# Grouped attention in a new order: scores of the next head first, queries three heads ahead, output tiles spread over three heads

## The reference

```
bsz, q_len, _ = hidden_states.shape          # 2, 512, 512 columns
q = (hidden_states @ wq.T)...                # 32 heads of 128
k = (hidden_states @ wk.T)...; v = ...       # 8 heads of 128, each shared by 4 query heads
q = q * cos + _rotate_half(q) * sin
k = k * cos + _rotate_half(k) * sin
scores = jnp.einsum('bhqd,bhkd->bhqk', q, k) / math.sqrt(HD)
scores = scores * scale                      # 0.5 or 1.5 for some key columns
scores = scores + causal
probs = jax.nn.softmax(scores, axis=-1)
attn = jnp.einsum('bhqk,bhkd->bhqd', probs, v)
return attn @ wo.T
```

## Time and profile before

| what | value |
|---|---|
| median of 3 runs | 3551.32 us (3546.72 to 3552.46) |
| profiled execution | 3529.9 us, span 3528.1 us |
| TensorE | 2449.5 us busy, 69% |
| VectorE | 2231.0 us busy, 63% |
| ScalarE | 1390.7 us busy, 39% |
| GpSimd | 1191.0 us busy, 34% |
| mean granted clock of TensorE | 0.818 |
| weight units loaded | 442 of 256 KB |

### The profile page before, as it was taken

How to read it: one execution, slowest core, us unless ns; L and a number is a source line. 1 busy time by engine, 2 the same in 40 slices (tenths; PEclk the granted TensorE clock), 3 DMA queues, 4 the chain that set the end, 5 groups by cost and what they waited for, 6 DMA issues and landing times.

```text
span 3528.1 us, 32687 instructions
## 1 busy us (share of the span) xinstructions
PE 2449.5 (69%) x10360; PEld 1826.1 (52%) x10360; DVE 2231.0 (63%) x3359; ACT 1390.7 (39%) x2692; POOL 1191.0 (34%) x1040
## 2 busy tenths in 40 slices
PE   4885888466668467567888898888989765037026
PEld 3343377354456345446766676666767544036015
DVE  2734645798996699896435555535555444963973
ACT  1542612343431333442116555535555414713621
POOL 2020153421224421424554454545545303044030
PEclk8896998587889578778989999999999868568557
DMA  5121121202001301101221111111111001012000
GB/s 184 46 98 66 63 74 36 90 12 75 24 18 42 90 15 38 49 24 45 78 65 34 39 45 37 48 45 39 44 39 45 30 12 48 0 45 60 0 21 24
DMA packets 97434, 167.00 MB, mean 47 GB/s; under 512 B 8952, under 2 KB 25848, under 8 KB 97144
## 3 DMA queue, kind: packets, MB, share of 16 engines
q1 hardware_dynamic: 97272, 164.98, 15.0%
HBM read 149.74 MB, written 14.81 MB: 47 GB/s over the span
## 4 chain that ended last, share of the span: by engine, by line
PE 29%; DVE 15%; issue 6%; ACT 3%; POOL 2%; DVEq 0%; POOLq 0%; ACTq 0%
PE ps L562 25%; PE ps L576 3%; DVE k L1503 3%; DVE g L1390 1%; ACT g L1046 1%; DVE g L1369 1%; ACT g L1040 1%; POOL w_lo L513 1%; DVE k L1549 1%; DVE g L1377 1%; POOL g L533 1%; POOL g L538 1%; DVE m L1333 1%; ACT g L1061 1%; DVE g L1376 1%
## 5 line engine op out<-in xcount | busy, mean ns | idle before, releaser
L512 POOL TENSOR_SCALAR w_hi<-w_in 128x512 fp32r<-128x512 f32 x442 | 338.4, 766 | 1450.0 <-PE ps L562 849.1
L513 POOL TENSOR_TENSOR w_lo<-w_in,w_hi 128x512 fp32r<-128x512 f32 x442 | 641.4, 1451 | 36.8
L562 PE MATMUL ps<-m,const_sb 128*128 128x256 f32 x1024 | 353.8, 506 | 324.9 <-DVE m L1345 324.8
L562 PEld LDWEIGHTS ps<-m,const_sb 128*128 128x128 f32 x1024 | 249.2, 253 | 418.6 <-DVE m L1345 243.5
L562 PE MATMUL ps<-hT_hi,w_lo 128*128 128x512 f32 x864 | 358.4, 415 | 22.6 <-issue 7.2
L562 PE MATMUL ps<-hT_lo,w_hi 128*128 128x512 f32 x864 | 345.2, 400 | 0.0
L562 PE MATMUL ps<-hT_hi,w_hi 128*128 128x512 f32 x864 | 343.3, 397 | 0.0
L1006 ACT ACTIVATE m<-m_rows,negA 128x256 f32<-128x256 f32 x512 | 215.6, 497 | 252.7 <-DVE m L1333 186.6
L1333 DVE TENSOR_TENSOR_SCAN m<-m,m 128x1028 f32<-128x1028 f32 x128 | 309.6, 2419 | 8.5 <-ACT m L1006 4.8
L576 PE MATMUL ps<-const_sb,k 128*128 128x128 f32 (+1 forms) x88 | 15.5, 312 | 360.4 <-POOL k L522 360.4
L562 PE MATMUL ps<-g,g 128*128 128x128 f32 (+3 forms) x704 | 197.1, 416 | 26.2 <-ACT g L1053 17.1
(11 more groups left out here) (208 smaller groups left out, 5489.5 us busy)
## 6 DMA issues: line engine op xcount, KB each, us to landing
w_in<-units SPq DMA_DIRECT2D x442, 256.0 KB, 2.6
m<-bc_scratch SPq DMA_DIRECT2D x32, 512.0 KB, 6.8
stack_scratch<-a SPq DMA_DIRECT2D x48, 256.0 KB, 3.0
a<-stack_scratch SPq DMA_DIRECT2D x128, 96.0 KB
x_sb<-x SPq DMA_DIRECT2D x2, 1024.0 KB, 7.6
out<-x_sb SPq DMA_DIRECT2D x2, 1024.0 KB, 4.2
small_sb<-small SPq DMA_DIRECT2D x1, 1399.0 KB, 12.5
const_sb<-consts SPq DMA_DIRECT2D x1, 708.0 KB, 7.0
```

Source lines behind the costliest of these rows:

```text
L512: c["did"](nc.gpsimd.tensor_scalar(w_hi[:, r], raw, 1.0, 1.0, ALU.mult, ALU.mult), s["unit_hi"])
L513: c["did"](nc.gpsimd.tensor_tensor(w_lo[:, r], raw, w_hi[:, r].bitcast(F32), ALU.subtract), s["unit_split"])
L562: ins = T.matmul(out, lhsT, rhs, start=start, stop=stop)
```

## The change

One function, `gqa_units`, now gives both the order of the weight units and a table `free`: how many units are released when GpSimd comes to the entry of a key or query. GpSimd splits up to that number + 8 (before: the entry's place in the order + 7). For the second head of a group the number is lower by five, since the four output units, and the query that lies behind them, are still held.

TensorE's round h becomes: scores(h+1); transposes(h); projection of query h+3, with the first output tile or tile 2 behind it, or with tile 3 ahead of it, or with the key of two groups on behind it; values(h); in the first round of a group output tile 1 at the end. So a group's output tiles are spread over three rounds: 0 and 1, then 2, then 3. They all use bank 3. The kept values have 6 slots instead of 4. Key 1 is projected ahead of the rounds. ScalarE and VectorE are ordered to match: ScalarE takes the exponentials of h+1 in round h, VectorE the maxima and norms of h+1 in round h, the rotation of query h+2, and that of key g+3 in the first round of a group. ScalarE no longer waits for its own exponentials and copies, and VectorE not for its copy and low part.

The diff, cut:

```diff
+def gqa_units():
+    names = [("gv", i) for i in range(2 * HC)] + [("gk", 0), ("gq", 0), ("gk", 1), ("gq", 1), ("gq", 2)]
+    free = {name: n + 1 for n, name in enumerate(names)}
+    for h in range(GH):
+        held = h % G_REP == 1 and h > G_REP
+        if h + 3 < GH:
+            names.append(("gq", h + 3))
+            free[names[-1]] = len(names) - (1 + G_REP if held else 0)
+        if h % G_REP == 0 and h:
+            names += [("go", h - G_REP + r) for r in range(G_REP)]
+        if h % G_REP == 3 and h // G_REP + 2 < G_KV:
+            names.append(("gk", h // G_REP + 2))
+            free[names[-1]] = len(names)
+    return names + [("go", GH - G_REP + r) for r in range(G_REP)], free
...
-                    names = item_units(it)
-                    for k, name in enumerate(names):
+                    names, free = gqa_units()
+                    for name in names:
                         if name[0] not in ("gk", "gq"):
                             continue
 
-                        split_units(first_unit[n] + min(k + RING - 1, len(names)))
+                        split_units(first_unit[n] + min(free[name] + RING, len(names)))
...
                 project(claim_rope(7), ("gq", 0), b, s["g_q"])
+                project(claim_rope(3), ("gk", 1), b, s["g_k"])
                 project(claim_rope(7), ("gq", 1), b, s["g_q"])
...
-                def out_rows(g, tiles):
-                    if 0 in tiles:
+                def out_rows(g, t):
+                    if t == 0:
-                    for t in tiles:
-                        o = claim(g_out_bank[t], s["x_added"])
-                    if TT - 1 in tiles:
-                        release(G_REP)
+                    o = claim(3, s["x_added"])
+                    for r in range(G_REP):
+                        hi, lo = unit(("go", g * G_REP + r), r)
...
+                def project_ahead(bank, name, sem, ahead):
+                    hi, lo = unit(name, ahead)
+                    o = claim_rope(bank)
+                    for k in range(HC):
+                        w = slice(k * P, (k + 1) * P)
+                        mm3(o, hi[:, w], lo[:, w], hT_hi[:, b, k], hT_lo[:, b, k], k == 0, k == HC - 1, sem if k == HC - 1 else None)
                 scores(0)
+                project(claim_rope(7), ("gq", 2), b, s["g_q"])
                 for h in range(GH):
-                    if h % G_REP == 1 and h > 1:
-                        out_rows(h // G_REP - 1, [TT - 1])
-                    if h:
-                        values(h - 1)
-                    if h + 2 < GH:
-                        project(claim_rope(7), ("gq", h + 2), b, s["g_q"])
-                    if (h + 3) % G_REP == 0 and h + 3 < GH:
-                        project(claim_rope(3), ("gk", (h + 3) // G_REP), b, s["g_k"])
+                    g, part = h // G_REP - 1, h % G_REP
+                    if h + 1 < GH:
+                        scores(h + 1)
                     for t in range(TT):
                         turns(h, t)
-                    if h + 1 < GH:
-                        scores(h + 1)
-                    if h % G_REP == 0 and h:
-                        out_rows(h // G_REP - 1, range(TT - 1))
-                values(GH - 1)
-                out_rows(G_KV - 1, range(TT))
+                    if part == 2 and g >= 0:
+                        out_rows(g, 3)
+                        release(G_REP + (1 if h + 2 < GH else 0))
+                    if h + 3 < GH:
+                        if part == 1 and g >= 0:
+                            project_ahead(7, ("gq", h + 3), s["g_q"], G_REP)
+                        else:
+                            project(claim_rope(7), ("gq", h + 3), b, s["g_q"])
+                    if part < 2 and g >= 0:
+                        out_rows(g, 2 * part)
+                    if part == 3 and g + 3 < G_KV:
+                        project(claim_rope(3), ("gk", g + 3), b, s["g_k"])
+                    values(h)
+                    if part == 0 and g >= 0:
+                        out_rows(g, 1)
+                for t in range(TT):
+                    out_rows(G_KV - 1, t)
+                release(G_REP)
...
+                    if h >= G_KEEP:
+                        act.wait_ge(s["g_out"], TT * (b * G_KV + (h - G_KEEP) // G_REP + 1))
+                    elif b:
+                        act.wait_ge(s["g_out"], TT * G_KV * b)
+                    go(A(g_a_hi[:, h % G_KEEP], ps[:, 6], ACT.Copy), s["g_hi"])
...
+                for t in range(TT):
+                    exp(0, t)
                 swap(7)
                 for h in range(GH):
-                    exp(0)
-                    exp(1)
-
-                    late = h % G_REP == 1 and h > 1
-                    if h and not late:
-                        keep_values(h - 1)
-                    exp(2)
-                    exp(3)
                     for t in range(TT):
                         norm(t)
-                    if late:
+                    if h:
                         keep_values(h - 1)
-                    keep_turned(1)
-                    keep_turned(2)
-                    if h + 2 < GH:
+                    for t in range(1, TT):
+                        keep_turned(h, t)
+                    if h + 1 < GH:
+                        for t in range(TT):
+                            exp(h + 1, t)
+                    if h + 3 < GH:
                         swap(7)
-                    if (h + 3) % G_REP == 0 and h + 3 < GH:
+                    if h % G_REP == 3 and h // G_REP + 2 < G_KV:
                         swap(3)
-                    keep_turned(3)
-                    heads_done["g"] += 1
...
+                times_cos(g_kc, 3, s["g_k"])
+                times_cos(g_qc, 7, s["g_q"])
+                rope_k(1)
+                rope_q(1)
+                maxima_1()
+                maxima_2()
+                times_cos(g_qc, 7, s["g_q"])
+                norms(0)
+                norms(2)
...
+                for h in range(GH):
+                    g, part = h // G_REP - 1, h % G_REP
+                    if part == 1 and g >= 0:
+                        add(1)
                     if h + 1 < GH:
-                        rope_q(h + 1)
-                    norms(0)
-                    if adds:
-                        add(1)
-                    norms(2)
-                    if adds:
-                        add(2)
-                        add(3)
+                        maxima_1()
+                    keep_turned(h)
                     if h:
                         values_low(h - 1)
-                    keep_turned(0)
+                    if h + 1 < GH:
+                        maxima_2()
+                    if part == 2 and g >= 0:
+                        add(3)
                     if h + 2 < GH:
+                        rope_q(h + 2)
+                    if part == 0 and h and g + 2 < G_KV:
+                        rope_k(g + 2)
+                    if h + 3 < GH:
                         times_cos(g_qc, 7, s["g_q"])
-                    if (h + 3) % G_REP == 0 and h + 3 < GH:
+                    if part < 2 and g >= 0:
+                        add(2 * part)
+                    if part == 3 and g + 3 < G_KV:
                         times_cos(g_kc, 3, s["g_k"])
-                    if (h + 2) % G_REP == 0 and h + 2 < GH:
-                        rope_k((h + 2) // G_REP)
-                    done["g"] += 1
+                    if h + 1 < GH:
+                        norms(0)
+                        norms(2)
                 values_low(GH - 1)
                 for t in range(TT):
                     add(t)
```

More of the change, by code:

```diff
@@ L59 @@
 G_RING = 3
+G_KEEP = G_REP + 2
 def unit_names():
@@ L140, in item_units @@
     if kind == "gqa":
-        out = [("gv", i) for i in range(2 * HC)] + [("gk", 0), ("gq", 0), ("gq", 1)]
-        for h in range(GH):
-            if h + 2 < GH:
-                out.append(("gq", h + 2))
-            if (h + 3) % G_REP == 0 and h + 3 < GH:
-                out.append(("gk", (h + 3) // G_REP))
-            if h % G_REP == 0 and h:
-                out += [("go", h - G_REP + r) for r in range(G_REP)]
-        return out + [("go", GH - G_REP + r) for r in range(G_REP)]
+        return gqa_units()[0]
     if kind == "topk":
@@ L306, in hybrid_layers @@
         g_bank = [(0, 0), (0, P), (1, 0), (2, 0)]
-        g_out_bank = [6, 3, 7, 3]
         g_pT = cut("g", TT * L, TT)
-        g_a_hi, g_a_lo = cut("g", G_REP * L, G_REP, F32R), cut("g", G_REP * L, G_REP, F32R)
+        g_a_hi, g_a_lo = cut("g", G_KEEP * L, G_KEEP, F32R), cut("g", G_KEEP * L, G_KEEP, F32R)
         g_max, g_sh, g_sum, g_inv = cut("g", TT), cut("g", TT), cut("g", TT), cut("g", TT)
@@ L825, in values @@
                            kt == 0, kt == TT - 1, s["g_values"] if kt == TT - 1 else None)
-                def out_rows(g, tiles):
-                    if 0 in tiles:
+                def out_rows(g, t):
+                    if t == 0:
                         need(s["g_lo"], G_REP)
```

(33 more changed lines are left out.)

15 lines of the change are left out of this document (6 added, 9 removed).

## The result

The changed kernel takes 3575.91 us (median of 6 runs) where the kernel before takes 3548.55 (6 runs): a ratio of 1.0088, 95% interval 1.0059 to 1.0118. The medians are 27 us apart, and the ratio makes it 31. The forecast was 44 us slower.

The account below looks back on a forecast made before the run. TensorE leads, so only its waits pay. Terms +20.0 + 2.6 + 14.5 - 8.8 - 9.0 + 2.7 = +22.0 a batch, +44 on 3529.9: 3574, median 21.4 above: 3595 us; own range 3565 to 3619, 8 in 10: 3525 to 3632.

Parts of the forecast that it names:

- Steady groups: Five uncut groups of four heads per batch: 62.0 us each against 58.0, together +20.0.
- the cut one: Sixth group, cut in two by the batch's ends: 33.4 for rounds 4 and 5, 27.2 for 26 and 27; 60.6, +2.6.
- the stall before the scores: TensorE waits 2.6 to 3.8 us for query 4g+1, rotated only after GpSimd's burst of six splits in a row.
- the tile's: TensorE waits 5.5 us before output tile 1, because tile 0's addition stands behind the key's rotation on VectorE.
- the key's rotation: VectorE's rotation of a key with scaled copies: taken as 4.3 us, 5.3 in the old trace.
- the price of the clock behind the tile: Low TensorE clock after the stall before output tile 1: 2.5 us a group, the middle of 1.7 and 3.5.
- Start of a batch: First key's projection to the mark of head 0: 39.5 us against 25.0, +14.5.
- First heads: Heads 0 to 3, without output tiles: 39.6 us against 48.4, -8.8.
- Last heads: Heads 28 to 31, with neither key nor burst of splits: 31.8 us against 40.8, -9.0.
- End of a batch: Last four tiles share one bank, three wait for additions: +3.0, less 0.3 for a warmer end, +2.7.
- all waits hidden: Rival: TensorE becomes the bound, 48.6 us a group, -57 a batch, 3437 in all; chance 0.15.
- burst hidden, key not: Rival: six splits begin by 6.4, query 9 in time, group 56.7, batch -8.6, 3534 in all; chance 0.12.

Follow-up runs that it names:

- Experiments 4 and 5: Changed kernel plus one unused GpSimd subtraction, behind the six splits (4) or in query 4g's entry (5): 3575.2 and 3568.4 us, single runs.
- experiment 1: Changed kernel with the key's rotation last in its round on VectorE: 3493.7 us, 0.9880 of the kernel before.
- experiment 2: Changed kernel with two GpSimd splits, not six, ahead of query 4g+1's rotation, the other four in the next entry: 3555.4 us, 1.0036 of the kernel before.
- Experiment 8: On top of experiment 7, the start of a batch as in the kernel before: 3431.0 us, 0.9698 of the kernel before.
- experiment 7: Changed kernel with the key's rotation in the next round and two splits, not six, ahead of query 4g+1: 3438.6 us, 0.9741 of the kernel before.
- Experiment 9: On top of Experiment 8, the copy of the first transpose on ScalarE instead of VectorE: 3402.9 us, 0.9611 of the kernel before.

## Why the prediction was right

It was right in direction and in its two stalls, and its number (3595) lies 19 us from the measured 3576. By its own steps, the first batch in the trace of after:

- *Steady groups and the cut one, from head 4 to 28.* Forecast +22.6 a batch, measured 369.7 - 348.1 = +21.6. That this is so close is in part luck, since two misses cancel: the five steady groups were put at +20.0 and are +17.5, the cut one at +2.6 and is +4.1. In the steady groups the stall before the scores was put at 2.6 to 3.8 and is 2.6; the tile's was put at 5.5 and is 4.3 to 5.1 (5.04 in the group shown); the key's rotation at 4.3 and is 4.2; the price of the clock behind the tile at 2.5 and is 5.14 - 2.82 = 2.3. Experiments 4 and 5 show that GpSimd's burst is on the path, experiment 1 that the key's place is, experiment 2 that the first alone gives most of it back. In the cut group the scores of head 29 wait twice as long, 5.29, with the low clock behind it: the round before them has no key's projection, which takes 2.8 elsewhere, so TensorE comes to them that much earlier. Rounds 26 and 27 were put at 27.2, without their parts, and take 28.7. The scores behind this stall take 4.2 instead of 2.3, and the sum names no low clock behind a stall of the scores.

```profile
2292.06 0.90 PE L571 MATMUL ps<-g,g 128*128 128x128 f32 x3 [5.29 <-POOL g L547]
```

- *Start of a batch.* Forecast +14.5, measured 39.5 - 25.0 = +14.5 in batch 0. Experiment 8 takes 11 to 12 of it away, and shows that half of that comes back in the rounds behind.
- *First heads.* Forecast -8.8, measured 39.4 - 48.4 = -9.0.
- *Last heads.* Forecast -9.0, measured 30.0 - 40.8 = -10.9. The gain was put too small: the three rounds take 14.7, 8.8 and 6.5 where the forecast had 15.8, 9.2 and 6.8. The forecast doesn't break these down, so which part was too long stays open.
- *End of a batch.* Forecast +2.7, measured +0.2 (head 31 to the next batch's first key projection: 43.8 against 43.5). The three waits for the shared bank are there: 0.78 each, of which 0.69 is the addition, and the four tiles take 14.4 instead of 11.3. The step "less 0.3 for a warmer end" was mis-sized: from the mark of head 31 to the first tile the new end takes 2.9 less. The old one has its values at the low clock (4.63 for what takes 2.4 after), which is 2.2 of it; the rest is shorter waits and transposes ahead of the values.

Together +16.5 in batch 0. Batch 1 has +20.2 from its first key's projection to the mark of head 31, more than batch 0 (its groups from head 4 to 28 grew by 24.6). That is 37 in the attention, where 44 was forecast and the ratio says 31. The two spans themselves are 53.3 apart, but 15.8 of that lies ahead of the first key's projection, where nothing was changed: the execution profiled after was a long one, 3583.2 against the median of 3576. The terms that missed by most lie at the end of a batch. The larger of them is mostly the clock of a stretch in which I had priced the pieces without asking what TensorE did just before.

The rival "all waits hidden" fell; it named its condition, though: query 4g+1 rotated by 20.5 and the key by 28.6. Experiments 7 and 9 don't meet it to the letter, as they move the key out of the way, but they show what hiding the waits brings: 51.6 and 49.1 a group. The rival "burst hidden, key not" was put at 3534 with the group at 56.7; experiment 2, which comes nearest to it, gave 60.7 and 0.5%. That rival had the splits begin earlier, and so query 4g+2 in time as well; the spread only hands the late splits to its entry.

GpSimd beside VectorE behaved in the trace of after as the prediction took it: with GpSimd silent the third operation of the key fell from 1.37 to 0.29. But I used it for the key alone. That it would hold the maxima, and with them the copy that TensorE's transposes wait for, I saw only as a late copy in one round. Experiment 9 shows that taking this copy out of VectorE's queue was worth 0.9% of the kernel once the larger waits were gone. That GpSimd is what made the copy late rests on the rows shown under experiment 7; no run takes GpSimd's work away there.

## What to carry to other kernels

A new order for the busiest engine is only as good as the three queues that have to follow it: walk each of them for a round, and look for what stands behind an instruction that waits, and whether the thing that frees a buffer is behind it. Stalls in series can hide each other: here removing the first alone gave 0.5%, the second alone 2.1%, both together 1.8% in one place of the key and 3.4% in another. So try the pair together, and in a place where the second can't grow. Where an engine has two jobs, one urgent and short and one long and early (a rotation, a batch of splits), try putting no more of the long one ahead of the short than is needed next.

## What the runs showed of the hardware

- GpSimd beside VectorE: an addition with two SBUF operands of 128 columns took 1.24 instead of 0.29, a scaling of 2 columns 0.86 instead of 0.17, each ending 0.03 to 0.16 behind an instruction of GpSimd (experiment 7); in the trace of after an operation of 128 columns took 1.17 in the same way. Here a short operation was held for several times its own length.
- TensorE's clock: a stall of 5.0 has the low clock behind it in the group of the changed kernel read above (5.14 for what takes 2.82; the granted clock is 0.94 in both groups shown), and no such stretch follows the 1.78 of experiment 1. One of 2.57 went either way in one and the same kernel. In experiment 1 it stands ahead of the scores in both of these groups. Behind the first (2022.17) the scores run at full clock; behind the second (2077.34) they begin at full clock and fall to the low one, 0.68 up to 2081.00. The groups' granted clocks are 1.00 and 0.97:

```profile
1998.15:2053.33 55.18, 48.26 (x242) 38.40 (x240) 32.21 (x72) 29.37 (x74) 29.13 (x27) 1.00 0.15 44
2053.33:2108.52 55.19, 49.29 (x242) 39.52 (x240) 32.25 (x72) 29.34 (x74) 29.15 (x27) 0.97 0.15 44
```
